# mLSTM in a fused tower kernel: contractions as full and half row groups, maxima spread by ScalarE, another order in a pair

## The reference, cut to what matters

```python
xz = x @ W_up                                   # 192 -> 576
x_mlstm, z = jnp.split(xz, 2, axis=-1)          # 288 each
xc = causal_depthwise_conv4(x_mlstm) + conv_b   # along the 36 tokens
x_conv = jax.nn.silu(xc)
q, k = x_conv @ Wq, x_conv @ Wk
v = x_mlstm @ Wv
h = _mlstm_cell(q, k, v, Wi, bi, Wf, bf, norm_w)  # gates from [q, k, v]; decays, scores, head norm
h = (h + skip * x_conv) * jax.nn.silu(z)
return h @ W_down                               # 288 -> 192
```

## Time and profile before

| | |
|---|---|
| median of 3 runs | 2581.3 us (2573.34 to 2583.25) |
| profiled execution | 2577.02 us, span 2575.2 us |
| TensorE matmul busy / weight load busy | 2179.4 us (85%) / 1915.3 us (74%) |
| VectorE, ScalarE, GpSimd busy | 1490.0, 872.2, 905.3 us (58%, 34%, 35%) |
| granted TensorE clock, mean | 0.881 |
| this stage | from about 57.5 to 420 us of the span |
| from the first `scores` to the last | 94.89 to 396.83 us: ten periods, 301.94 us |

### The profile page before, as it was taken

One profiled execution on the slowest core, in us unless ns is written; L12 is line 12 of the kernel. 1 busy time (PEld: TensorE's weight loads), 2 busy tenths in 40 slices (PEclk: granted clock), 3 DMA queues, 4 the chain that ended last, 5 costly groups with the idle time before them and its releaser, 6 DMA issues. The chain is left out here.

```text
span 2575.2 us, 46822 instructions
## 1 busy us (share of the span) xinstructions
PE 2179.4 (85%) x17545; PEld 1915.3 (74%) x17545; DVE 1490.0 (58%) x3843; ACT 872.2 (34%) x1874; POOL 905.3 (35%) x834
## 2 busy tenths in 40 slices
PE   7999996679869965997899989998999996663598
PEld 7888884467758864996677668887999996552487
DVE  1667776746667864632899863333444336777434
ACT  0333434722234422333555531111111113676211
POOL 0223224710020043554656630230233331473546
PEclk9989896789979956998999999998999998755599
DMA  9900000081000043552000005012666652000354
GB/s 257 204 1 1 1 1 20 1 187 43 2 1 2 2 168 119 184 187 81 16 11 11 1 1 214 26 41 78 230 210 213 214 194 59 6 1 1 114 173 124
DMA packets 117734, 218.79 MB, mean 85 GB/s; under 512 B 14028, under 2 KB 89753, under 8 KB 110725
## 3 DMA queue, kind: packets, MB, share of 16 engines
q1 hardware_dynamic: 106596, 195.13, 24.6%
q0 software_dynamic: 10912, 20.67, 2.5%
HBM read 164.63 MB, written 51.11 MB: 84 GB/s over the span
## 5 line engine op out<-in xcount | busy, mean ns | idle before, releaser
L2615 POOL COPY bl_swiglu_w<-ahead_w2swiglu_w 128x1152 f32 x51 | 58.2, 1144 | 272.3 <-PE psum L2675 213.4
L2717 ACT ACTIVATE bl_swiglu_sg<-psum 128x384 f32<-128x384 f32 x102 | 50.1, 491 | 303.3 <-PE psum L2664 303.3
L2653 PE MATMUL psum<-bl_swiglu_xt,bl_swiglu_w 128*128 128x128 f32 x1224 | 147.4, 278 | 2.2 <-DVE bl_swiglu_hid L2770 1.6
L2653 PEld LDWEIGHTS psum<-bl_swiglu_xt,bl_swiglu_w 128*128 128x128 f32 x1224 | 145.5, 194 | 2.8 <-issue 2.8
L2744 DVE COPY bl_swiglu_xt<-psum 128x256 f32<-128x256 f32 x51 | 21.6, 424 | 198.0 <-PE psum L2634 198.0
L2131 POOL DMA_INDIRECT rows_in<-tower_h,tower_spots x66 | 65.2, 988 | 173.4 <-DVE tower_spots L3068 140.0
L2729 ACT ACTIVATE bl_gelu_hid<-psum,bl_gelu_w 128x128 f32<-128x128 f32 x258 | 71.3, 377 | 111.0 <-POOL bl_gelu_w L2615 108.2
L2675 PE MATMUL psum<-bl_swiglu_w,bl_swiglu_hid 128*128 128x192 f32 x612 | 107.9, 326 | 0.0
L2675 PEld LDWEIGHTS psum<-bl_swiglu_w,bl_swiglu_hid 128*128 128x128 f32 x612 | 98.3, 190 | 0.1
L2930 PE MATMUL psum<-tower_xT,shared_w 128*128 128x256 f32 x432 | 96.4, 379 | 0.6 <-ACT tower_xT L2994 0.6
L3000 ACT ACTIVATE shared_sg<-psum 128x512 f32<-128x512 f32 x54 | 32.2, 597 | 187.8 <-PE psum L2937 187.8
(11 more groups left out here) (682 smaller groups left out, 6109.0 us busy)
## 6 DMA issues: line engine op xcount, KB each, us to landing
bl_swiglu_w<-in_swiglu_w SPq DMA_DIRECT2D x51, 1152.0 KB, 5.1
bl_gelu_w<-in_gelu_w SPq DMA_DIRECT2D x43, 576.0 KB, 4.3
bl_relu_w<-in_relu_w SPq DMA_DIRECT2D x25, 576.0 KB, 4.0
rows_in<-tower_zeros SPq DMA_DIRECT2D x1, 14065.0 KB, 61.4
rows_in<-tower_zeros SPq DMA_DIRECT2D x1, 13968.0 KB, 59.8
ahead_w2swiglu_w<-in_swiglu_w SPq DMA_DIRECT2D x1, 9216.0 KB
tok_x<-in_x SPq DMA_DIRECT2D x11, 648.0 KB, 12.5
ahead_w2gelu_w<-in_gelu_w SPq DMA_DIRECT2D x1, 5400.0 KB
```

Of the source, the lines that this page charges most:

```text
L2615: pool.tensor_copy(w2[:, n % DEEP], w2all[:, e, :].rearrange("p e n -> p (e n)")).then_inc(s_w2, 1)
L2653: pe.matmul(up_tile(n, j, i, side), w[:, o:o + 128], xt[:, n % 2, side, :], start=(i == 0), stop=False, skip_group_check=True)
L2717: act.activation(sg[:, j], bank_pair(n, j)[:, 0, 0:3 * BLOCK].rearrange("p (i n) -> p i n", i=3), ACT.Silu).then_inc(s_silu, 1)
```

## The change

- Contractions over 192 channels become one matmul over 128 rows and one over 64 rows (`hT` holds channels 0 to 127 and 64 to 191); those over 288 become two over 128 and one over 32. Matmuls over the short remainders are written one after another with alternating row groups and different PSUM banks. This holds for `up` (outputs in six groups of 128, the third with four copies of the last 32 channels) and `project`; `output` has 128, 128 and 32 rows for each tile.
- `values` no longer reads `xm`: `wuv`, the product of `wup` and `wv`, is formed once at the start (six matmuls and a copy), and `values` contracts `hT` with it over 128 + 64 rows.
- All tiles between have 128 rows rather than 96; transposes take blocks of 128 channels. The gates' bias is added by VectorE as it reads PSUM, not by a row of ones.
- `spread_peaks` moves from GpSimd (two multiplications on 8 rows) to ScalarE (four activations on 128 rows with a scale per row); the constants of `right` now lie in `gm`, so the loads shrink from 432 + 216 KB to 108 + 2 KB, while `wup` grows from 432 to 768 KB and `wq` and `wk` by 64 KB each; there are three more DMAs.
- Order. TensorE: after `queries(p+1)` now `turn_back(p)`, `turn(p+2)`, `keys(p+1)`, `output(p)`, `up(p+2)`. VectorE: `normalise(p)` ahead of `forget(p+1)`, `gated(p)` ahead of `decay(p+1)` and `keys(p+1)`, `add(p)` ahead of `conv(p+2)`. ScalarE: `spread_peaks(p+1)` between `turned(p+2)` and `raised(p+2)`. `thresholds` uses bank 3.

```diff
@@ gpsimd
                 def products(p):
                     pool.wait_ge(c_xs, MC * (p + 1))
                     pool.wait_ge(c_sz, p + 1)
-                    if p:
-                        pool.wait_ge(g_r, p)
...
-                def spread_peaks(p):
-                    pool.wait_ge(g_y, p + 1)
-                    pool.wait_ge(g_m, 2 * p + 2)
-                    for a in range(2):
...
@@ tensor
-                            ins = pe.transpose(bank(0)[0:CH, o:o + T], h[:, 2 * p + u, k * CH:(k + 1) * CH], ident[0:T, 0:T])
+                            ins = pe.transpose(bank(0)[:, o:o + T], h[:, 2 * p + u, 64 * k:64 * k + 128], ident[0:T, 0:T])
...
+                    def out(m):
+                        b, half = ((0, 0), (0, 1), (1, 0), (2, 0), (4, 0), (4, 1))[m]
+                        return bank(b)[:, half * C:half * C + C]
                     for m in range(2 * MC):
...
-                        for k in range(2):
-                            ins = pe.matmul(bank((0, 1, 4)[m // 2])[0:CH, o:o + C], wup[:, k, m * CH:(m + 1) * CH], hT[0:CH, p % 2, k, :],
-                                            start=(k == 0), stop=(k == 1))
-                        if m % 2:
-                            ins.then_inc(p_up, 1)
+                        side = m in (2, 4, 5)
+                        pe.matmul(out(m), wup[:, side, m * 128:(m + 1) * 128], hT[:, p % 2, side, :],
+                                  start=m not in (1, 5), stop=False, skip_group_check=True)
+                    for pair_of in ((0, 2), (1, 4), (3, 5)):
+                        for side, m in enumerate(pair_of):
+                            r = slice(64 - 64 * side, 128 - 64 * side)
+                            ins = pe.matmul(out(m), wup[r, 1 - side, m * 128:(m + 1) * 128], hT[r, p % 2, 1 - side, :],
+                                            start=False, stop=True, skip_group_check=True)
+                            if m in (1, 2, 5):
+                                ins.then_inc(p_up, 1)
...
-                        for k in range(MC):
-                            ins = pe.matmul(bank(u)[0:T, 0:INNER], xm[:, k, cols(u)], wv[:, k, :], start=(k == 0), stop=(k == MC - 1))
+                        pe.matmul(bank(u)[0:T, 0:INNER], hT[:, p % 2, u, cols(u)], wuv[:, u, :], start=True, stop=False)
+                    for u in range(G):
+                        r = slice(64 - 64 * u, 128 - 64 * u)
+                        ins = pe.matmul(bank(u)[0:T, 0:INNER], hT[r, p % 2, 1 - u, cols(u)], wuv[r, 1 - u, :], start=False, stop=True)
...
+                            pe.matmul(out(0), wgx[:, 0, :], hT[:, p % 2, 0, :], start=False, stop=False, skip_group_check=True)
+                            pe.matmul(out(0), wgx[64:128, 1, :], hT[64:128, p % 2, 1, :], start=False, stop=False, skip_group_check=True)
+                    pe.wait_ge(c_xs, MC * (p + 1))
+                    for m in (0, 2, 1, 3):
+                        r = slice(32 * (m // 2), 32 * (m // 2) + 32)
+                        ins = pe.matmul(out(m), w[r, 2, m * 128:(m + 1) * 128], xs[r, 2, :], start=False, stop=True, skip_group_check=True)
...
+                            r = slice(96 if k == MC - 1 else 0, 128)
+                            ins = pe.matmul(bank(5)[0:T, u * D:u * D + D], y[r, k, cols(u)], wd[r, k, :], start=(k == 0), stop=(k == MC - 1))
...
+                for c in range(2):
+                    for m in range(MC):
+                        ins = pe.matmul(bank(6 + c)[:, 0:INNER], wupT[:, m, 64 * c:64 * c + 128], wv[:, m, :], start=(m == 0), stop=(m == MC - 1),
+                                        skip_group_check=True)
+                ins.then_inc(p_wuv, 1)
+                pe.wait_ge(s_wuv, 1)
                 values(0)
...
                         queries(p + 1)
-                        if p + 2 < NP:
-                            turn(p + 2)
-                        keys(p + 1)
                     turn_back(p)
                     if p + 2 < NP:
+                        turn(p + 2)
+                    if more:
+                        keys(p + 1)
+                    output(p)
+                    if p + 2 < NP:
                         up(p + 2)
-                    output(p)
@@ scalar
                 def raised(p):
-                    act.wait_ge(p_up, 3 * p + 1)
+                    act.wait_ge(p_up, 3 * p + 2)
                     act.copy(xm[:, 0:2], pair(0, 2)).then_inc(c_xm, 1)
...
+                def spread_peaks(p):
+                    act.wait_ge(g_m, 2 * p + 2)
+                    for j in range(4):
+                        ins = act.activation(right[:, :, j, :], gm[:].rearrange("p (u n) -> p u n", u=G), ACT.Identity, scale=pick[:, j:j + 1])
+                    ins.then_inc(g_r, 1)
...
                     if p + 2 < NP:
                         turned(p + 2)
+                    if more:
+                        spread_peaks(p + 1)
+                    if p + 2 < NP:
                         raised(p + 2)
@@ vector
-                    L.then(dve.tensor_copy(gf[:, 0], bank(4)[64:64 + NH, 0:C]))
+                    L.then(dve.tensor_scalar(gf[:, 0], bank(4)[64:64 + NH, 0:C], bif[64:64 + NH, 0:1], None, ALU.add))
...
                     variances(p)
+                    normalise(p)
                     if more:
                         forget(p + 1)
-                    normalise(p)
+                    gated(p)
                     if more:
                         decay(p + 1)
                         keys(p + 1)
-                    gated(p)
-                    if p + 2 < NP:
-                        conv(p + 2)
                     if p == NP - 1:
                         settle(1)
                     add(p)
+                    if p + 2 < NP:
+                        conv(p + 2)
```

More of the change, by code:

```diff
@@ L381, in weights_mlstm @@
     wgv = S.sb("wgv", [CH, MC, 128])
[L382 to L387, removed]
+    bif = S.sb("bif", [128, 1])
+    wd = S.sb("wd", [128, MC, D])
+    cw = S.sb("cw", [128, MC, 4])
+    cb = S.sb("cb", [128, MC])
+    nw = S.sb("nw", [128, MC])
+    skip = S.sb("skip", [128, 1])
     first0 = S.sb("first0", [NH, C])
@@ L421, in stage_mlstm @@
     with Stage(nc, "ml", cst) as S:
-        (wup, wupT, wq, wk, wv, wqT, wkT, wvT, wgq, wgk, wgv, wgx, wd, cw, cb, nw, skip, first0, firstneg,
-         left, right, pick) = cst["ahead"]["ml"]
+        (wup, wupT, wq, wk, wv, wqT, wkT, wvT, wgq, wgk, wgv, bif, wd, cw, cb, nw, skip, first0, firstneg,
+         left, gm, pick) = cst["ahead"]["ml"]
         wgm = S.sb("wgm", [CH, MC, 128])
         wmean = S.sb("wmean", [CH, MC * NH])
[L426 to L433, removed]
+        wgx = S.sb("wgx", [128, 2, 128])
+        wuv = S.sb("wuv", [128, 2, INNER])
+        hT = S.sb("hT", [128, 2, 2, C])
+        xm = S.sb("xm", [128, MC, C])
+        zr = S.sb("zr", [128, MC, C])
+        xc = S.sb("xc", [128, MC, C])
+        xs = S.sb("xs", [128, MC, C])
+        sz = S.sb("sz", [128, MC, C])
+        scale = S.sb("scale", [128, 2, MC, C])
+        shift = S.sb("shift", [128, 2, MC, C])
         vs = S.sb("vs", [T, 2, G, NH, DH + 1])
@@ L437, in stage_mlstm @@
         gf = S.sb("gf", [NH, 6, C])
-        gm = S.sb("gm", [128, C])
+        right = S.sb("right", [128, G, 4, T])
         thr = S.sb("thr", [T, G, NH])
@@ L457, in cols, with pair @@
             return slice(u * T, u * T + T)
-        def pair(b, n, rows=CH):
+        def pair(b, n, rows=128):
             return bank(b)[0:rows, 0:n * C].rearrange("p (m n) -> p m n", n=C)
@@ L651, in _ @@
                     for m in range(MC):
-                        ins = pe.matmul(bank(5)[0:CH, c * 128:c * 128 + 128], wupT[:, m, c * CH:(c + 1) * CH], wgm[:, m, :],
+                        ins = pe.matmul(bank(6 + c)[:, INNER:INNER + 128], wupT[:, m, 64 * c:64 * c + 128], wgm[:, m, :],
                                         start=(m == 0), stop=(m == MC - 1))
@@ L686, in turned @@
                     act.wait_ge(p_A, p + 1)
[L687 removed]
+                    act.copy(hT[:, p % 2], pair(0, 2)).then_inc(c_A, 1)
                 def raised(p):
[L690 removed]
+                    act.wait_ge(p_up, 3 * p + 2)
                     act.copy(xm[:, 0:2], pair(0, 2)).then_inc(c_xm, 1)
[L692 to L694 removed]
+                    act.copy(xm[:, 2], bank(1)[:, 0:C]).then_inc(c_xm, 1)
                     act.wait_ge(p_up, 3 * p + 3)
+                    act.copy(zr[:, 0], bank(2)[:, 0:C]).then_inc(c_z, 1)
                     act.copy(zr[:, 1:3], pair(4, 2)).then_inc(c_z, 1)
@@ L4462, in layout @@
     A["firstneg"] = np.tile(np.where(at % IMG == 0, -BIG, 0.0), (8, 1))
-    left, right, pick = np.zeros((128, G, T)), np.zeros((128, G, 4, T)), np.zeros((128, 4, T))
+    left, right, pick = np.zeros((128, G, T)), np.zeros((128, G, T)), np.ones((128, 4))
     spare = list(range(8, 32)) + list(range(40, 64))
@@ L4466, in layout @@
         left[a:a + 8] = -1.0
-        for j in range(4):
-            right[a + 32 + 2 * j + a // 64, :, j] = 1.0
```

(12 more changed lines are left out.)

108 lines of the change are left out of this document (48 added, 60 removed).

## The result

The changed kernel takes 2564.85 us (median of 7 runs, 2553.52 to 2568.26) against 2575.0 (7 runs), ratio 0.9944 [0.9926, 0.9961]. Its profiled execution took 2568.26 us, span 2566.5; it was the longest of the seven. The first scores come 1.1 us earlier (93.81 for 94.89), the last 9.0 us earlier (387.80 for 396.83).

The account below looks back on a forecast made before the run. TensorE was taken as close to the bound. A period of 28.1 us plus 1.05 for the clock gave 29.15 for 30.19; over ten periods, with the tenth somewhat more, -11.5: 2570 us on the median's scale, own range 2562 to 2578.

Parts of the forecast that it names:

- TensorE's list, 23.9: TensorE's work per pair with packed half and 32-row matmuls: 23.9 us against 26.35, 2.4 us less.
- rival "not packed": Halves are not packed where the two follow full ones closely: +2.0 us a pair, 2590 us; chance 0.07.
- `hn` at 15.4, a wait of 2.9: `hn` ready 15.4 us after the scores' start, 0.4 gained; TensorE waits 2.9 us before `turn_back`, after the queries.
- faster rival: VectorE slips through beside GpSimd's L484, `hn` comes 1.0 us earlier, the wait falls to 1.9: 2558 us; chance 0.21.
- Boundary, 1.5 on `thr`: Between up's end and the next scores, TensorE waits 1.5 us for the last copies and `thr`; the add's wait is gone.
- rival "no change": The convolution ends after 3.44 us, so silu, products, variances and `hn` slide one for one: 2581 us; chance 0.18.
- Steps "swallowed by the 2.9 us wait": `bits.step` and its like, 1 to 3 us in some pairs, push `weigh` and attend; the wait before `turn_back` absorbs up to that.
- The clock: Half-clock falls of 3.3 us behind the wait for `hn`, or at attend's end: 1.05 us a pair added.
- slower rival: The wait before `turn_back` costs the clock for 6.6 us, not 3.3, in every pair: +3.1 a pair, 2601 us; chance 0.12.
- Start, 0 within 2: At the stage's start, extra matmuls and a copy against savings and smaller loads: together 0, within 2 us either way.

Follow-up runs that it names:

- GpSimd's spreading: The changed kernel with the spreading of the maxima back on GpSimd, as four multiplications by a scale per row; ratio 0.9932 to the kernel before.
- long doses: The kernel with the steps ahead, plus 4, 6, 9 and 11 unread VectorE sums ahead of weigh in the second, fourth, sixth and eighth pair; ratio 0.9964.
- steps ahead: The changed kernel with VectorE's steps for later stages between add and convolution, the first levelling one pair earlier; 2536.9 us, ratio 0.9852.
- short doses: The kernel with the steps ahead, plus 2, 4, 6 and 8 unread VectorE instructions ahead of weigh in every second pair; ratio 0.9843.
- `hn` kernel: The boundary kernel with the next tiles' transposes ahead of those of `hn` and GpSimd's products held until `hn` is there; ratio 0.9820.
- boundary kernel: Steps ahead, plus up ahead of output, the add before the convolution's last tap, levelling halved over two pairs, scores' waits split by bank; ratio 0.9816.

## Why the prediction was right, and where not

2570 was forecast and 2564.85 came, inside the prediction's own range; against the kernel before, 11.3 us less were forecast (from 2581.3, the median of three) and 10.2 came (from 2575.0, the median of seven). The direction was right; the nearness is in part luck, for two errors cancelled: the full-clock period is 1.05 us shorter than forecast (28.1), and what lies above it is 2.35 us a pair instead of 1.05.

- *TensorE's list, 23.9.* It measures 24.9 (27.05 less 0.70 and 1.44); the terms themselves add up to 23.75, and those of the boundary's 1.5 to 1.65. Up took 3.68 for 3.5, values 1.95 for 1.7, queries 5.2 for 4.8, output with thresholds 2.94 for 2.6; keys (3.96 for 3.9) were met. Full matmuls of 216 columns behind a change of groups ran at 0.19 to 0.20 us rather than 0.183; that the change is the reason is not shown. Packing works (twelve halves in 1.30 us, where 0.183 each would be 2.2); the rival "not packed" is out.
- *`hn` at 15.4, a wait of 2.9.* Wrong: 14.0 and 0.70. The step that failed is the choice that GpSimd's one-input product holds VectorE as the two-input one does. Beside L483 the two-input L860 took 0.17; only L861 was held, till L483's end, and L865 till L484's. So the variances ended at 11.7 (L867) for 13.0, and the new order gave the 0.4 us that was forecast. This was the faster rival's mechanism, with 1.3 us for its 1.0. The prediction's own sign of being wrong, no wait before the transposes, is there in six of the ten pairs; in the four others the wait is 0.40 to 0.80 us.
- *Boundary, 1.5 on `thr`.* Right: 1.44. The spreading (1.57) is hidden, and the experiment shows that GpSimd could have kept it. The convolution ended at 3.1 (L806) for 3.3, so the rival "no change" is out.
- *Steps "swallowed by the 2.9 us wait".* The step that failed most. That wait was not there, and the steps lengthen others, to 4.26 and 3.94 us, with 5.8 and 17.2 us at about half clock near them. With the steps moved the ten periods took 28 us less: some 17 in the three periods about these two waits, 5 in the tenth, where attend had waited 1.17 us, and 5 in the falls of the first two pairs, which had no long wait and are not shown to come from the steps.
- *The clock.* The forecast's falls, behind the wait for `hn`, did not come, nor did the slower rival's. Those at attend's end did, in the first two pairs without a long wait. With the same instructions on TensorE, the clock fell in the first pair in three profiles (the changed kernel, GpSimd's spreading, the long doses) and not in two (steps ahead, short doses).
- *Start, 0 within 2.* Met: the first scores came 1.1 us earlier. TensorE's first transposes start 3.0 us earlier (55.71 for 58.75), with SyncE's wait for the last constant at 8.8 for 10.7; from there to the first scores the new list takes 2.0 us more, the new weights' product and its copy (3.9) among it.
```profile
SPq L327 <- DMA tower_smask<-in_smask: 8.8, 1, 8.8
```
*Open:* in which pairs the clock falls at attend's end. With wide matmuls between its halves none began there in the twenty pairs of two kernels; but with attend whole none began in the twenty of the steps-ahead kernel and the short doses either, so the split is not shown to be the reason.

## What to carry to other kernels

When an engine's work is moved behind another step, list what else is queued at its end: small steps for later stages that were covered before can become the longest waits. Read a gain in two parts, the full-clock period and the clock; here an order that leaves the full-clock period as it was gained as much as the whole change. A shorter list on the critical engine may not show until the next engine's queue is cleared: in the new order it paid 16 us of periods after that, and nothing that could be told from noise before. And profile a kernel whose time varies with the clock more than once before a fall is put down to an edit.

## What the runs showed of the hardware

GpSimd's instructions held some of VectorE's and not others. The Trainium skill (GPSIMD Engine Reference, Key points) says that GpSimd contends with VectorE instructions that have two SBUF inputs or run in a two-port mode. L865 (0.70 for 0.17) and the scan (1.89 for 0.60), two inputs each beside a two-input product, agree; L860, two inputs beside the one-input L483, was not held (0.17 to 0.18, in all eight pairs where it ran beside it), and L861, one input, was (0.64). Whether L861 ran in a two-port mode no run shows. In the `hn` kernel, with the products held back, the same three took 0.17 to 0.18.

A run of 32 matmuls of 37 columns (3.2 us) was followed by a clock of 0.50 for 6.4 us or a little more, with no wait above 0.38 us near, in four of nine full pairs of the boundary kernel, which cost 2.5 to 3.0 us each; in the steps-ahead kernel the same run was followed by no fall in ten.
